# Four front phases put into one stage in component order, and held weights in the second experts' first products

## The reference

```python
mod = (silu(L0_c) @ L0_wmod)                  # sa, ca, ga, sb, cb, gb; the gates are kept from zero
h = layernorm(x) * (1 + ca) + sa
q = (h @ Wq).reshape(T, 16, 16); k = h @ Wk; v = h @ Wv       # 16 heads share one k and one v
scores = einsum('ihd,jd->hij', q, k) / 4, causal mask, softmax
x = x + ga * (einsum('hij,jd->ihd', attn, v).reshape(T, 256) @ Wo + bo)
x = x + gb * experts0(...)                    # top 1 of 8, capacity 320
x = x + ga1 * mixer(...)                      # layer 1
h = layernorm(x) * (1 + cb1) + sb1
# experts1: top 2 of 8; per expert e, F = 512:
y = (silu(h @ w1[e].T) * (h @ w3[e].T)) @ w2[e].T
x = x + gb1 * sum over the two chosen experts of coef * y
```

## Time and profile before

| | |
|---|---|
| median of 3 runs | 1245.53 us (1245.0 to 1249.11) |
| the profiled execution | 1249.32 us |
| its span in the profile | 1247.6 us, PE at a mean of 0.895 of its full clock |
| front (setup to the end of the projection) | 0 to 571.7 us |
| second experts' blocks | 1001 to 1231.7 us |

### The profile page before, as it was taken

The page is one execution under the profiler, slowest core; times in us unless marked ns, Lnnn a source line. Parts: engine busy times, 40 slices in busy tenths (PEclk is TensorE's granted clock), DMA queues, the critical chain, the costliest instruction groups (busy, mean ns, idle before and its releaser), DMA issues. The chain is left out here.

```text
span 1247.6 us, 23402 instructions
## 1 busy us (share of the span) xinstructions
PE 982.1 (79%) x9002; PEld 567.3 (45%) x9003; DVE 671.2 (54%) x1764; ACT 493.1 (40%) x792; POOL 306.9 (25%) x367
## 2 busy tenths in 40 slices
PE   4632899999999999896069999518567599999994
PEld 1420244444445445263047767413345556666662
DVE  3843999999999999155300000198775612122121
ACT  1320066767767767844022222063126422222220
POOL 2003011021021021132412222135820034444441
PEclk9775599999999999997569999859778899999998
DMA  5299700000000000006414555300036622232233
GB/s 190 44 145 132 105 3 2 3 3 2 3 2 3 3 3 3 2 1 198 178 39 111 160 127 144 80 0 1 1 90 231 220 43 44 45 46 46 42 46 84
DMA packets 79690, 81.88 MB, mean 66 GB/s; under 512 B 22800, under 2 KB 71568, under 8 KB 79344
## 3 DMA queue, kind: packets, MB, share of 16 engines
q1 hardware_dynamic: 65200, 61.44, 19.4%
q0 software_dynamic: 12288, 17.10, 8.3%
q10 hardware_dynamic: 2112, 2.10, 0.5%
HBM read 58.45 MB, written 24.13 MB: 66 GB/s over the span
## 5 line engine op out<-in xcount | busy, mean ns | idle before, releaser
L566 ACT ACTIVATE prob<-p_s 128x1024 f32<-128x1024 f32 (+3 forms) x320 | 269.0, 894 | 109.8 <-PE p_s L509 109.6
L497 PE MATMUL p_p<-k_ks,k_qs 112*32 112x512 bf16 (+3 forms) x2560 | 227.3, 374 | 58.7 <-PEq L270 38.9
L591 DVE TENSOR_REDUCE mpart<-p_p 128x1 f32<-128x512 f32 x384 | 248.9, 684 | 8.7 <-PE p_p L497 7.0
L509 PE MATMUL p_s<-k_qs,k_ks 114*32 114x512 bf16 (+3 forms) x2560 | 177.3, 349 | 5.7 <-ACT prob L566 2.9
L497 PEld LDWEIGHTS p_p<-k_ks,k_qs 112*32 112x32 bf16 x2560 | 76.1, 95 | 177.2 <-DVE mpart L591 67.2
L524 PE MATMUL p_o<-prob,k_vaug 128*32 128x512 f32 (+3 forms) x1280 | 147.6, 529 | 2.5 <-DVE k_oT L608 1.9
L684 POOL TENSOR_SCALAR_AFFINE_SELECT prob<-prob 128x256 f32<-128x256 f32 x128 | 51.7, 408 | 361.0 <-ACT prob L566 359.6
L588 DVE CUSTOM_DVE_ANT_0 unread<-p_p,causal 128x128 bf16<-128x128 f32 (+3 forms) x256 | 120.5, 484 | 6.9 <-PE p_p L497 4.6
L509 PEld LDWEIGHTS p_s<-k_qs,k_ks 114*32 114x32 bf16 x2560 | 73.5, 97 | 83.8 <-issue 27.4
L1869 DVE TENSOR_TENSOR mid<-silu_g,e_u 128x512 f32<-128x512 f32 x39 | 26.8, 687 | 138.7 <-PE e_u L1763 138.7
L1358 DVE SCALAR_TENSOR_TENSOR outr<-p_o,rows,k_mod 128x256 f32<-128x256 f32 x16 | 7.7, 484 | 141.5 <-PE p_o L1315 141.5
(11 more groups left out here) (284 smaller groups left out, 1267.8 us busy)
## 6 DMA issues: line engine op xcount, KB each, us to landing
r_raw<-in_L_ffn_w_dram SPq DMA_DIRECT2D x24, 512.0 KB, 6.0
k_wi<-in_L_ffn_wi_dram SPq DMA_DIRECT2D x8, 1024.0 KB, 5.1
k_wo_e<-in_L_ffn_wo_dram SPq DMA_DIRECT2D x8, 1024.0 KB, 7.3
k_qs<-q_dram SPq DMA_DIRECT2D x28, 256.0 KB, 9.4
sum<-k_x SPq DMA_DIRECT2D x8, 512.0 KB, 6.8
wmod<-in_L_wmod_dram SPq DMA_DIRECT2D x2, 1536.0 KB, 12.2
q_dram<-q_parts SPq DMA_DIRECT2D x12, 256.0 KB, 13.1
disp<-zeros SPq DMA_DIRECT2D x2, 1310.0 KB, 19.3
```

The source lines that it names most:

```text
L497: last = nc.tensor.matmul(p1[n % 3][32 * j:32 * (j + 1), 0:w], k.qs[0:KROWS, qt // TQ, GH * G + hs, q0:q0 + 32], k.ks[0:KROWS, QC * ck:QC ...
L509: last = nc.tensor.matmul(sc[pair][32 * j:32 * (j + 1), i, off:QC], k.ks[0:KALL, k0:k0 + 32], k.qs[0:KALL, c, GH * g + 2 * pair + i, off:Q ...
L566: nc.scalar.activation(prob[:, u % 2, 2 * pair:2 * pair + 2, off:QC], sc[pair][:, :, off:QC], ACT.Exp, scale=HD ** -0.5).then_inc(e_done, 1)
L591: nc.vector.reduce_max(mpart[:, hs, qt, ck:ck + 1], p1[n % 3][:, 0:w], AX.X).then_inc(p1_used, 1)
```

## The change

**One front stage.** `phase_front` replaces the four phases. Its groups are (c, g), component outside, so 16 groups of 4, 8, 12 or 16 units: still 160 units and 640 chunks. `front_schedule` writes out which chunks go with which unit: 40 (`PRE`) ahead of the first unit, then two to five a unit, each group's last one at least four units (`MARGIN`) ahead of its first unit. Chunks, v products, modulation rows and the three steps of the output projection ("A" transposes, "B" transposes, "C" product) go through one ring of three PSUM banks. The remainders of q and k are formed on PE, by a bf16 product with minus the identity into the same PSUM (`take_away`), and ACT cuts all parts; scale and shift are applied by ACT as it copies the transposes. The output copy moves from DVE to ACT. The gate is folded into Wo, the bias is added to x by POOL, and DVE adds the product to x.

**Spill by heads.** The columns of Wq are put in the order (d, h), and `q_dram` is [component, part, 256, 512], so each of the 16 partitions of a load reads one run of 16 KB; the first component is loaded in two pieces, group 0's heads first.

**Second experts.** w1 and w3 of the block's expert are copied into double buffers (by ACT and by DVE) and are the held weights of the first products, which come out with the hidden index on partitions. `e_m` and its copy are gone; `e_y` has two banks.

```diff
-            for n in range(PER_U * LEAD):
-                first_pass(0, n)
-            for g in range(NG):
-                group(g)
+            for u, (s, kt) in enumerate(units):
+                mine, more = per_unit[u]
+                if kt == 0:
+                    pe.wait_ge(rows_in[s], 16 * NROWDMA)
+                scores(u, 0)
+                for r in mine[0:1]:
+                    entry(r)
+                scores(u, 1)
+                for r in mine[1:3]:
+                    entry(r)
+                if u:
+                    values(u - 1)
+                for r in mine[3:] + more:
+                    entry(r)
...
+            def take_away(c, step, j):
+                pe.wait_ge(part_done, 9 * c + 3 * step + j + 1)
+                piece = ks[:, QC * c:QC * (c + 1)] if j == 2 else parts[:, c % 2, step, j, :]
+                nc.tensor.matmul(pj[j], minus[:, 1 + step if j == 2 else 0, :], piece, start=False, stop=True,
+                                 skip_group_check=True).then_inc(pj_done, 1)
...
-                     k.q_dram[part, :, QC * c:QC * (c + 1)].rearrange("(h d) n -> d h n", d=HD)).then_inc(k.q_in[c], 16)
+                                 k.q_dram[c, part, :, :].rearrange("(d h) n -> d h n", d=HD)[:, h0:h1, :]).then_inc(landed, 16)
...
-                nc.vector.tensor_copy(k.oT[:, g, QC * c:QC * (c + 1)], ot[:, :]).then_inc(o_copied, 1)
+                nc.scalar.copy(oT[:, c % 2, g, :], ot[:, :]).then_inc(o_copied, 1)
...
-            def product(out, s, e, mat, done):
-                for t in range(KH):
-                    last = nc.tensor.matmul(out[:, :], xT[:, s, t, :], k.w1T[:, e, mat, 512 * t:512 * (t + 1)],
-                                            start=(t == 0), stop=(t == KH - 1))
+            def product(out, s, w, done):
+                for c in range(FT):
+                    for t in range(KH):
+                        last = nc.tensor.matmul(out[:, P * c:P * (c + 1)],
+                                                w[:, s, F1 * t + P * c:F1 * t + P * (c + 1)],
+                                                xT[:, s, t, :], start=(t == 0), stop=(t == KH - 1))
                 last.then_inc(done, 1)
...
-                for f in range(FT):
-                    last = nc.tensor.transpose(pm[:, P * f:P * (f + 1)], m[:, s, P * f:P * (f + 1)], k.ident[:, :])
-                last.then_inc(mt_done, 1)
...
+            def gate_weights(i, s):
+                e = act.value_load(k.block_expert[0:1, bass.ds(2 * i + s, 1)], min_val=0, max_val=E - 1)
+                nc.scalar.copy(wg[:, s, :], k.w1T[:, e, 0, :]).then_inc(wg_ready, 1)
...
+            def up_weights(b):
+                e = dve.value_load(k.block_expert[0:1, b:b + 1], min_val=0, max_val=E - 1)
+                nc.vector.tensor_copy(wu[:, b % 2, :], k.w1T[:, e, 1, :]).then_inc(wu_ready, 1)
```

More of the change, by code:

```diff
@@ new lines, in _ @@
+            act.wait_ge(wq_in, 16 * 3)
+            for t in range(KH):
+                nc.scalar.copy(wqd[:, t, :].rearrange("p (d h) -> p d h", d=HD),
+                               wq[:, t, :].rearrange("p (h d) -> p d h", d=HD)).then_inc(wqd_ready, 1)
+            act.wait_ge(col_ready, 2)
+            act.wait_ge(const_in, 16 * 2)
+            copy_turned(0)
+            for c in range(NC):
+                for j in range(3):
+                    piece(c, 0, j)
+                if c + 1 < NC:
+                    copy_turned(c + 1)
+                for step in range(1, 3):
+                    for j in range(3):
+                        piece(c, step, j)
@@ new lines, in _ @@
+            for r in range(NPRE):
+                entry(r)
+            for u, (s, kt) in enumerate(units):
+                c, g = groups[s]
+                off = max(0, kt - TQ * c) * P
+                if u >= 2:
+                    act.wait_ge(pv_done, u - 1)
+                for pair in range(2):
+                    act.wait_ge(s_done, 2 * u + pair + 1)
+                    nc.scalar.activation(prob[:, u % 2, 2 * pair:2 * pair + 2, off:QC], sc[pair][:, :, off:QC],
+                                         ACT.Exp, scale=HD ** -0.5).then_inc(e_done, 1)
+                if u - 1 in last_unit:
+                    copy_out(last_unit[u - 1])
+                for r in per_unit[u][0] + per_unit[u][1]:
+                    entry(r)
@@ L218, in _ @@
+            copy_out(NS - 1)
+            for r in per_unit[NU][1]:
+                entry(r)
         @block.vector
@@ new lines, in _ @@
+            rstd_after = {u: n for n, u in enumerate([max(v for v in range(NU) if ("C", TQ * c + TQ - 1) in
+                                                          [entries[r] for r in per_unit[v][1]]) + 1 for c in range(NC - 1)])
+                          for u in [u]}
+            for u, (s, kt) in enumerate(units):
+                if u == 5:
+                    fold_gate()
+                if u >= 6 and u % 2 == 0 and u < 14:
+                    add_bias((u - 6) // 2)
+                if u in rstd_after:
+                    ln_rstd(nc, pool, k, rstd_after[u], var2_ready, rstd2_ready)
+                if u in diags:
+                    off = (kt - TQ * groups[s][0]) * P
@@ L1821, in _ @@
             e = expert_of(NB - 1)
-            back(PAIRS, 0, False)
-            second(PAIRS, 0, e, False)
+            second(PAIRS, 0, e)
         @block.scalar
```

1079 lines of the change are left out of this document (509 added, 570 removed).

## The result

The changed kernel takes 1195.24 us (median of 4 runs, 1191.96 to 1198.01) where the kernel before took 1246.51 beside it (4 runs, 1245.0 to 1249.11): ratio 0.959, 95% interval 0.956 to 0.962. The forecast of 1193 and its range hold.

The account below looks back on a forecast made before the run. The front has stretches with different limits, DVE and PE both near theirs in the longest; PE alone bounds the second experts. Front -36 us and experts -16.7 give -52.7, so 1193 us for the median; 8 in 10 within 1174 to 1216.

Parts of the forecast that it names:

- Experts: Second experts: without `e_m` a block takes 5.38 us for 5.82, at 0.108 us a pass; -16.7 us over 38 blocks.
- (a): Front, start to first chunk: first projection at 17 us, 11.1 us a component, parts done at 64, cold 67.
- the rival of the low clock: Front: PE stays at clock 0.50 in projection and chunks, first unit near 125, total 1215 likely; 15 in 100.
- (b): Front, to the first unit: 32 more chunks and six modulation products, 20 us; first unit taken at 91.
- the cold case: Front, before the first unit: PE's clock falls to 0.50, the modulation products take 20.6 us, first unit at 98.
- (c): Front, query loads: 122 GB/s, 15 us a component, ending near 97, behind the projection whatever the piece size.
- the 4 us that I put at the fourth unit: Front: second group's maxima rows, behind the last component's loads in SP's order, may cost 4 us there.
- (d): Front, chunks beside units: DVE needs 361 us and PE 339 by pace; 376 to 390 expected, 386 taken.
- Its sign of being wrong: Front, last component's units: ACT or PE ahead of DVE in the profile would show the forecast wrong.
- (e): Front, units alone: 20 units as now, 39.6 us, plus 3 for ACT's copies and PE's four tiles; 43 us.
- (f): Front, end: four projection tiles instead of 16, so 30.7 us becomes 12.
- The rival of loads that aren't hidden at all: Second experts: weight load and pass follow one another, 3.42 us a product, +115 us, total 1325; 6 in 100.

## Why the prediction was right, step by step

**The sum.** Front 536 against 571.7, -36: the router starts at 536.0 where it started at 572.96, -37.0 (alone its ratio is 0.969). Experts -16.7: some -12 (11.7 alone). Together -52.7 forecast, -51.3 in the medians.

**(a) Start and components.** Taken one by one: the forecast had the first projection at 17, 11.1 us a component, the parts done at 67 and the first chunk near 55. Measured were 21.67; 12.6, 12.9 and 11.2; some 69.4; and 61.66. The 11.1 was right in its mechanism: a component at full clock takes 11.2 (47.11 to 58.29). Two things were mis-sized. DVE and ACT begin with work that waits for the last small load, 13.08 us, of which putting the statistics first gives back 2.0. And the granted clock falls in this stretch: 0.73 from 36 to 40 us in the changed kernel, 0.50 in the kernel with the front alone, whose component from 29.75 to 44.27 takes 14.5 us (12.9 in the changed kernel). The stretches, the changed kernel's first:

```profile
36.00:40.00 4.00, 4.00 (x8) 1.56 (x7) 0.00 (x0) 0.94 (x2) 0.00 (x0) 0.73 0.60 141
```

```profile
36.00:40.00 4.00, 4.00 (x10) 2.45 (x10) 0.23 (x1) 0.00 (x0) 0.00 (x0) 0.50 0.56 135
```

That is the rival of the low clock, in a small part: 1.4 to 3.3 us in a component, not 30 in all. For the first component's 1.4 us the granted clock reads 1.00, but its first three matmuls take 2.90 us (rows above), where eight take 3.68 at 47.11; that is the pace of the lower level. Other traces of this front have 0.50 to 1.00 at 36 to 40 us, and with that first chunks from 60.76 to 65.22.

**(b) To the first unit.** 91 forecast, 94.83 measured. Of the 3.8 us, 2.4 are those of (a); the rest is 25.4 us from there on for the 24 of the forecast (20, and 4 allowed for the clock). The granted clock stayed at 0.94 in this stretch, where chunks alone had run at 0.50, so the 98 of the cold case didn't come. That the six products among the chunks keep it up is argued; no run takes them out.

**(c) The queries.** Right on what carried the sum: the loads are behind the projection, and the pieces don't matter. The rate is 134 GB/s for 122. But the reason that I leaned to, the 16 partitions of a load, is only partly borne out: two sets at once brought nothing. And the 4 us that I put at the fourth unit had the wrong cause and size. The last loads cost a gap of 3.73 us at the third unit, by holding PE up in the middle of a product and not by making the maxima rows late, and 1.8 us of it reach DVE's row. In the sum the 4 us stand as 91 + 4 = 95, and the first unit came at 94.83 because it started late, by (a) and (b). That the sum is met there is luck.

**(d) Chunks beside units.** 386 forecast, 94.83 to 480 measured, 385. Here the experiments say more than the sum did: the stretch is, at least up to some 400 us, one row of DVE's work that starts with the first chunk. An error in the first unit's time does not add up with it, as 3.5 us more there cost nothing. So the forecast's order of terms (first unit, then 386) was right by its total and wrong as a chain. Its sign of being wrong, PE ahead of DVE in the last component's units, can't be ruled out by the busy shares from 400 us on; the forecast had itself reckoned PE's pace as the larger there.

**(e), (f).** 43 and 12 forecast; 44 (480 to 524; the last maxima are made at 480.94) and 12.2 (523.80 to 536.0) measured.

**Experts.** The failed size is the pass, 0.108 forecast ("the pace is the larger") and 0.1116 measured, inside the bound of 0.116. The larger limit is the load, not the columns, as the run with half the columns shows: I had read the load's price from `p_v` as 0.106, and it is 0.108 to 0.112 in a row of products. 0.13 us more for the two products together, by 38 blocks, is 4.9 us, the 5 that are missing (16.7 forecast, 11.7 measured alone). The rival of loads that aren't hidden at all is refuted: 0.214 a pass would have been 3.42 us a product. (The break-even of 0.155 us a pass that stands with this rival is a slip: 36 us over 39 blocks come to 0.151.) The rule that the prediction weighed from the Trainium skill, "TensorE: Matmul & The Clock Gate", Part 3, "The mechanism", that a load overlaps a matmul only when its row group differs, does not hold for this case: 0.1116 us for load and pass of all rows.

## What to carry to other kernels

When two engines are both near 96% busy in a long stretch, find the one without slack by delaying the start of the other's work: some 3.5 us for PE's units cost nothing here, while gate and bias work taken off DVE's row showed with 3 to 4 us. Hold such traces against ones that started alike: the clock alone moved the first chunk by up to 4.5 us. And what a stop of PE costs goes by what the pacing engine has to do meanwhile: 3.22 us beside DVE's gate work cost 0.1, and 4.14 where DVE waited for chunks cost 5. Held weights that remove a transposition give what it took, less what their loads cost above the columns: 0.44 less 0.13 us a block here, because at 128 fp32 columns the load already sets the pace. And the first dimension of a transfer decides how many DMA engines serve it: a broadcast of three copies as the first dimension cost 85 us.

## What the runs showed of the hardware

- Weight loads of 128x128 fp32 set the pace of a product at 0.108 to 0.112 us a load, with 64 moving columns as with 128.
- Transfers with a first dimension of 2 or 3 used 0.13 of the 16 DMA engines and moved 53 GB/s, 25 per busy engine; 16 engines on 16 partitions moved 134, 8.4 each.
- Large loads held PE up in the middle of a product with no semaphore pending, for 2.9 to 4.6 us in the seven traces where they lay beside the third unit; issued later, they did it there, for 2.1 and 4.1 us. That it is instruction fetch is not shown.
- DVE's operation of 0.17 us took 1.80 beside a POOL addition of 2.37 us. The reverse shows in the experts: POOL's gather issue takes 1.17 us beside DVE's new copy of weights, 0.98 before:

```profile
1027.86 1.17 POOL L1903 DMA_INDIRECT xb<-h_rows,k_tok_of  x1 [1.67 <-PE e_x L1754]
1028.22 0.69 DVE L1859 COPY wu<-k_w1T 128x1024 f32 x1
```

- The granted clock of the same stretch differs between executions: 0.50, 0.65, 0.73, 0.93 or 1.00 at 36 to 40 us, 1.00 in the changed kernel and 0.50 in the one with half the columns at 970 to 980 us.
